# Float32 queries and keys on 32-row tiles of TensorE, in place of stacked bfloat16 parts

## What is computed

```python
q, k, v = split_heads(x @ Wq + bq), split_heads(x @ Wk + bk), split_heads(x @ Wv + bv)   # layer 1: no biases
attn = q @ k.T / sqrt(16) + slopes[h] * (key - (T - 1))      # layer 1: no such slope
attn = where(causal, attn, min_float32)
x = x + (softmax(attn) @ v) @ Wo + bo
```

## Time and profile before

| | us |
|---|---|
| median of 3 runs | 438.63 |
| lowest, highest | 436.79, 441.16 |
| span of the profiled execution | 441.7 |

### The profile page before, as it was taken

The page is one execution under the profiler, slowest core; times in us unless marked ns, Lnnn a source line. Parts: engine busy times, 40 slices in busy tenths (PEclk is TensorE's granted clock), DMA queues, the critical chain, the costliest instruction groups (busy, mean ns, idle before and its releaser), DMA issues.

```text
span 441.7 us, 14528 instructions
## 1 busy us (share of the span) xinstructions
PE 410.0 (93%) x6328; PEld 237.2 (54%) x6328; DVE 297.1 (67%) x596; ACT 232.9 (53%) x377; POOL 170.2 (39%) x250
## 2 busy tenths in 40 slices
PE   5799789999999988999999998998999999888997
PEld 5356564555555347544377466544555553465476
DVE  4636489999998216521336586899999981188883
ACT  3535355577776973221101541655877769635950
POOL 4107013314033144478692000234361544453770
PEclk9989799999999999999999997999999999999999
DMA  6899550000000000200100479400000000000002
GB/s 204 129 239 263 128 148 4 4 3 4 4 2 5 4 1 6 65 8 9 64 0 0 120 200 224 106 5 4 3 4 3 4 5 2 2 1 0 1 26 71
DMA packets 21657, 22.97 MB, mean 52 GB/s; under 512 B 2588, under 2 KB 20858, under 8 KB 21594
## 3 DMA queue, kind: packets, MB, share of 16 engines
q1 hardware_dynamic: 20498, 19.03, 17.8%
q0 software_dynamic: 544, 2.49, 1.9%
q10 hardware_dynamic: 552, 0.53, 0.4%
HBM read 8.27 MB, written 1.05 MB: 21 GB/s over the span
## 4 chain that ended last, share of the span: by engine, by line
PE 71%; DVE 14%; ACT 4%; DMA 3%; issue 3%; POOL 2%; SPq 2%; ACTq 0%; DVEq 0%
PE ps L785 11%; PE ps L765 11%; DVE mx L1258 11%; PE ps L743 10%; PE ps L916 8%; PE ps L1012 5%; PE ps L944 4%; PE ps L921 4%; ACT prob L1141 4%; PE ps L677 4%; PE ps L980 4%; DMA col_rows<-in_L_ffn_up_scale 3%; PE ps L845 3%; PE ps L751 2%; POOL xn L605 1%
## 5 line engine op out<-in xcount | busy, mean ns | idle before, releaser
L1258 DVE TENSOR_REDUCE mx<-ps 128x1 f32<-128x512 f32 (+3 forms) x304 | 181.1, 654 | 28.9 <-PE ps L751 24.1
L1141 ACT ACTIVATE prob<-ps 128x1024 f32<-128x1024 f32 (+1 forms) x192 | 145.4, 812 | 63.4 <-PE ps L765 63.1
L743 PE MATMUL ps<-kS,qS 96*32 96x512 bf16 (+21 forms) x1536 | 111.9, 321 | 4.4 <-DVE mx L1258 3.0
L590 POOL TENSOR_SCALAR_AFFINE_SELECT prob<-prob 128x256 f32<-128x256 f32 x128 | 51.9, 412 | 163.9 <-ACT prob L1141 162.5
L765 PE MATMUL ps<-qS,kS 101*32 101x512 bf16 (+7 forms) x1536 | 95.2, 326 | 3.7 <-ACT prob L1141 3.6
L785 PE MATMUL ps<-prob,v 128*32 128x512 f32 (+3 forms) x768 | 80.1, 489 | 0.6 <-POOL prob L590 0.4
L743 PEld LDWEIGHTS ps<-kS,qS 99*32 99x32 bf16 (+1 forms) x1536 | 42.8, 95 | 50.4 <-DVE mx L1258 28.1
L748 PE MATMUL ps<-mask_q,identb 128*32 128x32 bf16 (+1 forms) x1024 | 51.1, 186 | 2.7 <-issue 2.7
L765 PEld LDWEIGHTS ps<-qS,kS 101*32 101x32 bf16 (+1 forms) x1536 | 35.0, 96 | 31.2 <-ACT prob L1141 15.8
L751 PE MATMUL ps<-mask_q,identb 128*32 128x64 bf16 (+1 forms) x512 | 45.4, 198 | 0.0
L748 PEld LDWEIGHTS ps<-mask_q,identb 128*32 128x32 bf16 x1024 | 28.1, 98 | 14.0 <-issue 9.2
(11 more groups left out here) (146 smaller groups left out, 537.0 us busy)
## 6 DMA issues: line engine op xcount, KB each, us to landing
qS<-parts SPq DMA_DIRECT2D x24, 128.0 KB, 3.3
kS<-parts SPq DMA_DIRECT2D x24, 128.0 KB, 3.4
qS<-prob SPq DMA_DIRECT2D x12, 128.0 KB, 8.0
kS<-prob SPq DMA_DIRECT2D x12, 128.0 KB, 7.5
qS<-xn SPq DMA_DIRECT2D x12, 128.0 KB, 3.4
kS<-xn SPq DMA_DIRECT2D x12, 128.0 KB, 2.9
out<-x SPq DMA_DIRECT2D x8, 128.0 KB, 1.7
oT<-in_L_ffn_gate_w POOLq DMA_DIRECT2D x1, 768.0 KB, 4.8
```

What stands on the lines that cost most here:

```text
L590: nc.gpsimd.affine_select(out=square, in_=square, compare_op=ALU.is_ge, fill=0.0, base=0, pattern=[[0, 2], [1, P]], channel_multiplier=-1) ...
L743: mmi = nc.tensor.matmul(span[r:r + STRIP, 0:seen], qS[0:K_MAX[L], c, g * G + h, qt * P + r:qt * P + r + STRIP], kS[0:K_MAX[L], g * G + h, ...
L1141: nc.scalar.activation(prob[:, n % 3, 2 * pair:2 * pair + 2, off:CH], ps[:, 2 * (m % 2):2 * (m % 2) + 2, off:CH], ACT.Exp, scale=SCALE).th ...
L1258: ins = nc.vector.tensor_reduce(mx[:, slot, qt, heads[0]:heads[-1] + 1, part], src, AX_X, ALU.max)
```

## The change

- q and k are kept as float32, in one tensor qk of 32-row tiles: head l of group u lies on the row tile and slot that `place` gives, 16 rows of data, one more for the slope (layer 0), one more for the maximum.
- The weights of q and k are padded (wP), so that a projection lands on the tiles: 16 projections a layer in place of 8. Four are made ahead of the attention (QK_B), twelve as side jobs among the maxima, in the ring of the three maxima banks. ScalarE takes q out of PSUM with its bias, VectorE takes k and adds what was prepared in kS (bias and slope times position).
- The parts, their transfers and the six copies go. The maximum is one float32 row.
- `exp_scores`: the stationary operand is 128 keys on 17 or 18 rows, one float32 matmul for each head, a pair being heads of two row tiles. Only head 0 of layer 0 on the diagonal stays in strips of 32, for its mask.
- `max_scores`: 32 queries stationary as before, on 16 or 17 rows of the head's row tile. Items of one head follow HEADS = (0, 2, 1, 3), which alternates between two row tiles. Items never hold more than two heads.
- Side jobs have written places (`side_jobs`), counted in maxima. The turning of the feed-forward weights and layer 1's weights comes at maxima 64 to 114. GpSimd scales the integer weights between its triangles.

```diff
+SLOTS = 4
+QK_B = 4
+V_A = TPC
...
+def place(u, l):
+    return 2 * (u % 2) + l // 2, 2 * (u // 2) + l % 2
...
+def tile_rows(tile, n):
+    return slice(STRIP * tile, STRIP * tile + n)
...
+HEADS = (0, 2, 1, 3)
...
-        items += [(qt, 0, (h,), 0, CH * c) for qt in range(TPC) for h in range(G)]
+        items += [(qt, 0, (l,), 0, CH * c) for qt in range(TPC) for l in HEADS]
     for qt in reversed(range(TPC)):
         keys = P * (qt + 1)
-        per = CH // keys
-        items += [(qt, 1, tuple(range(h, h + per)), CH * c, keys) for h in range(0, G, per)]
+        if 2 * keys > CH:
+            items += [(qt, 1, (l,), CH * c, keys) for l in HEADS]
+        else:
+            items += [(qt, 1, (l, l + 1), CH * c, keys) for l in range(0, G, 2)]
...
+def side_jobs(L):
+    at = [(2, ("xnT",))] + [(4 + 2 * t, ("v", t)) for t in range(V_A)]
+    at += list(zip((13, 15, 18, 20, 25, 27, 30, 32, 50, 53, 56, 59), [("qk", n) for n in range(QK_B, N_QK)]))
+    at += [(38 + 3 * n, ("v", V_A + n)) for n in range(NT - V_A)]
+    if L == 0:
+        at += [(22, ("cols",)), (34, ("bias",))]
+        turns = [(w, k) for w in ("gateT", "upT", "downT") for k in range(HT // 2)]
+        at += [(64 + 3 * n, job) for n, job in enumerate(turns)]
+        at += [(96 + 6 * m, ("w1T", m)) for m in range(4)]
...
+            def projection_qk(L, bank, n):
+                c, slot, w = qk_job(n)
+                pe.wait_ge(a_free, A_AT["xnT", L, (c + 1) * TPC - 1] + 1)
+                for j in range(CJ):
+                    mmi = nc.tensor.matmul(bank[:, :], wP[:, L, w, j, slot], xnT[:, j, tokens(c)], start=j == 0, stop=j == CJ - 1)
+                return mmi
...
-                bank = ps[:, 4 + n % M_BANKS]
-                for i, h in enumerate(heads):
+                for i, l in enumerate(heads):
+                    tile, slot = place(u, l)
+                    rows, own = tile_rows(tile, K_MAX[L]), tile_rows(tile, STRIP)
                     span = bank[:, i * keys:(i + 1) * keys]
                     for r in range(0, P, STRIP):
-                        seen = keys if part == 0 or r == P - 2 * STRIP else keys - P + r + STRIP
-                        mmi = nc.tensor.matmul(span[r:r + STRIP, 0:seen], qS[0:K_MAX[L], c, g * G + h, qt * P + r:qt * P + r + STRIP],
-                                               kS[0:K_MAX[L], g * G + h, key0:key0 + seen], start=True, stop=part == 0)
+                        seen = keys if part == 0 else keys - P + r + STRIP
+                        mmi = nc.tensor.matmul(span[r:r + STRIP, 0:seen], qS[rows, c, slot, qt * P + r:qt * P + r + STRIP],
+                                               kS[rows, slot, key0:key0 + seen], start=True, stop=True)
...
-                    h = g * G + 2 * pair + i
+                    l = 2 * i + pair
+                    tile, slot = place(u, l)
+                    rows, own = tile_rows(tile, K_EXP[L]), tile_rows(tile, STRIP)
                     bank = ps[:, 2 * (n % 2) + i]
-                    masked = diagonal and L == 0 and h in STEEP
-                    for r in range(0, P, STRIP):
-                        mmi = nc.tensor.matmul(bank[r:r + STRIP, off:CH], kS[0:K_EXP[L], h, kt * P + r:kt * P + r + STRIP],
-                                               qS[0:K_EXP[L], c, h, off:CH], start=True, stop=not masked)
+                    masked = diagonal and L == 0 and u * G + l in STEEP
+                    wide = STRIP if masked else P
+                    for r in range(0, P, wide):
+                        mmi = nc.tensor.matmul(bank[r:r + wide, off:CH], kS[rows, slot, kt * P + r:kt * P + r + wide],
+                                               qS[rows, c, slot, off:CH], start=True, stop=not masked)
...
+            nc.vector.memset(wP[:, 0].rearrange("p m j s o -> p (m j s o)"), 0.0).then_inc(w0_zero, 1)
...
+                    for c in range(NC):
+                        for slot in range(SLOTS):
+                            chain(nc.vector.tensor_scalar(kS[:, slot, tokens(c)], pos[:, tokens(c)], hc[:, slot:slot + 1],
+                                                          bqk[:, 1, slot:slot + 1], ALU.mult, ALU.add))
```

More of the change, by code:

```diff
@@ L117, in ring_a_jobs @@
         jobs += [("xnT", L, t) for t in range(TPC, NT)]
[L118 to L123, removed]
+        jobs += [("v", L, t) for t in range(V_A)]
         gates = [("gate", L, c, ht) for c in FFN_C for ht in range(WHOLE[L])]
@@ L136, in ring_b_jobs @@
     for L in range(LAYERS):
-        jobs += [("qk", L, n) for n in range(N_QK)]
-        if L == 0:
-            jobs.append(("bias",))
+        jobs += [("qk", L, n) for n in range(QK_B)]
         ups = [("up", L, c, ht) for c in FFN_C for ht in range(WHOLE[L])]
@@ L152, in ring_b_jobs @@
         jobs += [("down", L, t) for t in DOWN_ORDER[L]]
+        jobs += [("none", L, n) for n in range(-len(jobs) % 4)]
     return jobs
 A_AT = {job: n for n, job in enumerate(ring_a_jobs())}
-B_AT = {job: n for n, job in enumerate(ring_b_jobs())}
+B_JOBS = ring_b_jobs()
+B_AT = {job: n for n, job in enumerate(B_JOBS)}
+B_FULL = {job: sum(j[0] != "none" for j in B_JOBS[:n + 1]) for n, job in enumerate(B_JOBS)}
+B_FREE = {job: sum(j[0] not in ("qk", "none") for j in B_JOBS[:n + 1]) for n, job in enumerate(B_JOBS)}
+HEADS = (0, 2, 1, 3)
 def max_items(c):
@@ L201, in attention_order @@
             entries.append(("max", cg, it))
+            n_max += 1
+            entries += [("side", job) for job in sides.get(n_max, [])]
             if waiting and n == T_LAG:
@@ L284, in alibi_tail @@
 def alibi_tail():
-    bf16 = mybir.dt.np(BF16)
     start = 2.0 ** -0.5
     slopes = np.array([start * start ** i for i in range(NH)], np.float32)
[L289 to L299, removed]
+    columns = np.zeros((P, N_HC), np.float32)
+    for h in range(NH):
+        tile, slot = place(h // G, h % G)
+        columns[STRIP * tile + HD, slot] = slopes[h] / np.float32(SCALE)
+    columns[HD::STRIP, HC_ONE] = 1.0
+    for L in range(LAYERS):
+        columns[K_MAX[L]::STRIP, HC_NEG[L]] = -1.0
+    return columns.view(mybir.dt.np(BF16))
 def two_layer_kernel(nc, a, out, tail):
@@ L735, in max_scores, with turn_cols, bias_product @@
-            def max_scores(L, n, cg, item):
-                g, c = CGS[cg]
+                return mmi
+            def turn_cols(bank):
+                pe.wait_ge(rows_in, 16 * 8)
+                return nc.tensor.transpose(bank[:, 0:N_COLS], col_rows[:], ident[0:N_COLS, 0:N_COLS])
+            def bias_product(bank):
+                pe.wait_ge(side_free, OTHER_SIDES.index(("cols",)) + 1)
+                pe.wait_ge(wvo_in, 16 * 2)
+                for j in range(CJ):
+                    mmi = nc.tensor.matmul(bank[:, 0:C], bv[:, j:j + 1].to_broadcast([P, P]), vo_w(0, 1)[:, j, :],
+                                           start=j == 0, stop=j == CJ - 1)
+                return mmi
@@ L753, in max_scores @@
-                mmi.then_inc(m_full, 1)
+                            mmi = nc.tensor.matmul(span[r:r + STRIP, keys - P + r:keys], identb[own, own], mask_m[own, own.start:own.start + P - r],
+                                                   start=False, stop=True, skip_group_check=True)
+                return mmi
             def exp_scores(L, s, pair):
-                g, c, kt, off, diagonal = step_span(s)
+                u, c, kt, off, diagonal = step_span(s)
                 n = 2 * (L * N_STEP + s) + pair
@@ L1090, in _ @@
+            act.wait_ge(w0_in[0], 16)
+            act.wait_ge(w0_zero, 1)
+            for j in range(CJ):
+                nc.scalar.copy(padded(wP[:, 0, 0, j]), heads_apart(w0[:, 0, j])).then_inc(w0_turned, 1)
             for L in range(LAYERS):
```

695 lines of the change are left out of this document (345 added, 350 removed).

## The result

The changed kernel takes 1062.27 us (median of 4, 1056.94 to 1074.19), the kernel before 439.37 in the same runs: a ratio of 2.42 (95% interval 2.40 to 2.43). The forecast was 688, its range ended at 790.

A forecast was written before the change was run, and what follows sets the result against it. TensorE's matmul stream alone was taken to bound the middle of each attention. Layer 0's +126.6 us and layer 1's +123 on the profiled 441.7 gave 691, less 3 for the median 688; range 530 to 790.

The forecast's parts named there:

- The sum: TensorE's matmul stream and changes of form in both attentions: 269.5 us in layer 0, 254.4 in layer 1.
- single items: Items of maxima standing alone, as most would (1.4 to 1.5 to a run); maxima 93.1 and 88.4 us a layer.
- changes of form: Switches of stationary shape on TensorE: 0.20 us into 128 columns, 0.12 into 32; 43.0 and 39.6 us a layer.
- The first maxima: Start of layer 0's maxima after four projections, forecast at 18.2 us where it was 36.7.
- VectorE's new work: Memset and eight passes over the keys' bias ahead of the first maxima: hidden, otherwise costing up to 4 us.
- floor of rival 1: Exponentials and maxima overlapping with every queue hole filled, no changes of form: 79.5 us a layer, 451 us in all.
- rival 1: Exponentials and maxima on different row tiles overlap: layers of 198 and 182 us, 547 us in all; chance 17%.
- exponentials and maxima do not overlap: In the attention's middle a change of form drains TensorE, so the two groups never run beside each other.
- rival 3: Sum holds but TensorE's clock sinks from waiting, or waits add up: a fifth at half clock, 790 us; chance 6%.
- The ramps: Attention starts (0 to 88, 241 to 308 us) where TensorE waits and its clock sinks to 0.91 and 0.79.
- Rival 2: Row tiles of 32 do not run side by side: 362 and 352 us a layer, 881 in all; chance 7%.
- Rival 4: Float32 scores stream cheaper on 32 rows: under 0.79 us per 512 columns ends below 438, 0.43 gives 411; chance 3%.

The follow-up runs named there:

- e6: Changed kernel with exponentials' scores, maxima and masks on tiles of 64 rows of dense data (output not attention's): 702.58 us.
- e1: Changed kernel with the exponentials' scores back in four strips of 32 keys, so exponentials and maxima have one form: 790.21 us.
- e11: Kernel before (bf16) with its scores and the maxima's masks on 32 rows in place of 96 to 101: 624.42 us, ratio 1.43.
- e5: Changed kernel with the exponentials' scores on all 32 rows of their row tile, the added rows holding zeros: 1057.16 us.
- e9: Changed kernel with the same tiles and forms, but 32 dense rows in each tile in place of 17 or 18: 999.42 us.
- e10: Like e7, everything on four row tiles in turn, but only 16 to 18 rows of each tile in use: 788.96 us.
- e2: Changed kernel with 16 more small bf16 matmuls on the whole array before each pair of exponentials' scores: 1269.72 us.
- e7: Changed kernel with all scores in 32 by 32 form, spread over four row tiles with 32 dense rows each (output not attention's): 599.2 us.
- e8: Changed kernel with q, k and the maxima each kept as one bf16 number in place of float32: 540.48 us.
- e3: Changed kernel with scores, maxima and masks on all 128 rows of the array, dense float32 operands (output not attention's): 860.37 us.

## Why the prediction was wrong

**The sum held.** Columns, pairs, single items, prices of float32 (0.86) and of a form (0.12 and 0.20), 280 and 261 changes of form (the timeline shows about 290 and 270): 524 us forecast, 547 measured in e6, which ran at the full clock, so 4% too little. The 520 of the changed kernel is length times clock and flatters the forecast: some 230 entries into 128 columns and 330 into 32 count in it as 0.15 and 0.075 us (half of 0.30 and 0.15) where they cost 0.20 and 0.13, about 30 us in all, and with them it is 550. Of the 23 us that the sum lacks, the forms' number and price give about 6; the rest was not traced. The first maxima came at 20.3 us, forecast 18.2, because the first projection starts at 13.2, not 11.2. The chain shows what lies ahead of it:

```profile
5.41 6.19 PE ps L1096 x60
11.60 0.24 PE ps L766 x2
```

L1096 is the warm-up. It ends at 11.6 us where it ended at 9.6 in the kernel before (59 records in 4.86 us from 4.78 on); why it took longer is open. VectorE's new work (L1386, 3.94 us from 8.19 on) begins after it has normalised the tokens that L766 turns, so it was hidden as forecast. One side sum does not follow from its terms: the floor of rival 1, 451 us. 79.5 with 31.0, 28.5 and 7 gives 452, and 462 with the masks' 5 in each layer.

**That exponentials and maxima do not overlap** held, for the reason given; e1 showed the overlap as soon as the forms are one. Rival 1's 547 us did not come even then: its work was 420, not 380, and its clock 0.64 to 0.68.

**The step that failed** is the clock. The sum prices all 524 us of the attentions at the full clock, on the strength of the sentence in rival 3, "The rows in full use show 1.00". The ramps had been read as the clock sinking where TensorE waits; that reading is not refuted for them, but it was taken as the only way for the clock to sink. In the stretches of the trace before that show 1.00, the scores and maxima take 96 to 101 rows of the array and most other matmuls 128, so they could not tell busy from full. The change keeps TensorE busier than before (467.1 of 467.2 us) and uses 17 or 18 rows of each tile, one or two tiles at a time. e11 shows the same fall in the kernel before with its scores and the maxima's masks on 32 rows, e6 shows it gone on 64 rows of dense data. The loss was placed in the right rival, with the right sign (a clock under 0.95 in the middle; it was 0.50 from 160 to 330 us), at 6% and for a fifth of the stream. Its cause there, TensorE having to wait, was the wrong one, and a mean of 0.58 between levels of 1.00 and 0.50 means the lower one for about 84% of the time. From 167 outside and 524 inside, a clock of 0.58 gives 167 + 524 / 0.58 = 1070.

The Trainium skill, TensorE: Matmul & The Clock Gate, Part 1, describes the gate as one that follows how busy the engine has been and names idle gaps as what costs the full clock. Read as busy time, this would have kept 1.00 here; the trace shows 0.58 with 0.12 us of idle time in 467, and the measurement decides.

**The other rivals.** Rival 2 (no company between row tiles of 32) is out: two items take 1.93 us as one does. Rival 4 (a cheaper stream on few rows) is out: 512 columns of float32 on 17 or 18 rows are 0.85 a record at half clock, 0.43 at full, as on 128.

**What stays open.** What exactly decides the clock was not measured. On the changed kernel's tiles, zeros on the exponentials' added rows brought nothing (e5, 0.641), dense rows in all scores 0.05 (e9), and turning over four tiles with 16 to 18 rows no more than e1 had without it (e10, 0.727 against 0.726). e2's whole-array filler of near-zeros and the long first fall of the changed kernel, 0.90, 0.69, 0.50, have no experiment of their own. Why e7's work is 441 us and not at most 380 was not looked into by a run of its own; a cause in the order of issue would be an argument only. No version here beats the kernel before: the fastest is e8, at 540, with an output only as good as bf16.

## What to carry to other kernels

Count the array's rows that carry data, not only the columns that stream: on a fraction of its rows a busy TensorE ran at half speed for most of two attentions here, and a form that needs more matmul time on more rows can be faster (e3 by 19%, with 35% more work). Before packing small matmuls into row tiles, see that several tiles with full rows are in flight at once (e7 at 1.00, e9 and e10 under 0.70 in the attentions), and that all that should overlap has one form, because each change of form waited for the stream before and cost 0.13 to 0.20 us at the full clock. A trace in which every stretch uses the whole array says nothing of the clock of a kernel that does not.

## What the runs showed of the hardware that was not expected

- The granted clock fell to its 1.2 GHz level under a TensorE that hardly paused: 0.58 in 467 us (0.12 us without a matmul) with scores on one or two row tiles of 17 or 18 rows, 0.54 in 224 us (1.7 without) with bf16 scores on 32 rows.
- As many matmuls of the same columns on tiles of 64 rows of dense data ran at 1.00, and so did 32 dense rows on four tiles in turn, where 16 to 18 rows had 0.68 and 0.64. Zeros on the exponentials' added rows changed nothing (0.641 against 0.637).
- Float32 and bf16 matmuls of one form (32x32 in e1) on different row tiles started inside each other's streams; in the changed kernel, in the stretch looked at, a matmul of another form did not.
- A change of form costs more at the lower clock, but not twice as much: 0.30 in place of 0.20 us into 128 columns, 0.15 in place of 0.13 into 32.
